# One chunk pair's operands stored quarter by quarter: how they lie in SBUF and how TensorE reads them

## The reference

```
mod = silu(c) @ wmod                      # sa, ca, ga, sb, cb, gb
h = layernorm(x) * (1 + ca) + sa
x = x + ga * attention(h)                 # 2 x 2 scores per feature over the batch
h = layernorm(x) * (1 + cb) + sb
x = x + gb * ((silu(h @ W_gate.T) * (h @ W_up.T)) @ W_down.T)
```

## Time and profile before

| | |
|---|---|
| median of three runs | 2774.9 us |
| the profiled execution's own time | 2773.0 us |
| its span (first to last instruction) | 2771.2 us |
| TensorE matmuls | 11640, busy 98% of the span |
| matmuls of the up projection (lines 1637 to 1639) | 3 x 2416 |
| VectorE, ScalarE busy | 66%, 47% |
| mean granted TensorE clock | 0.992 of 2.4 GHz |
| x_raw loads | 21 of 1024 KB |

### The profile page before, as it was taken

One profiled execution on the slowest core, in us unless ns is written; L12 is line 12 of the kernel. 1 busy time (PEld: TensorE's weight loads), 2 busy tenths in 40 slices (PEclk: granted clock), 3 DMA queues, 4 the chain that ended last, 5 costly groups with the idle time before them and its releaser, 6 DMA issues. The chain is left out here.

```text
span 2771.2 us, 32925 instructions
## 1 busy us (share of the span) xinstructions
PE 2708.4 (98%) x11640; PEld 2145.2 (77%) x11640; DVE 1816.6 (66%) x2503; ACT 1310.3 (47%) x2058; POOL 156.9 (6%) x206
## 2 busy tenths in 40 slices
PE   8989999998999999999999999999999999999999
PEld 3336888887888887888887888887888888888887
DVE  6979778865677766777766666556555555445444
ACT  4657455654456654465654333333433443343342
POOL 5300011000011000010000000000000000000000
PEclk9989999999999999999999999999999999999999
DMA  8683566649665649556658887787757657657655
GB/s 349 232 306 120 194 220 204 201 159 277 194 195 194 215 158 296 177 196 209 206 173 249 266 261 252 261 267 241 279 200 265 239 193 263 242 195 261 249 197 169
DMA packets 322595, 625.32 MB, mean 226 GB/s; under 512 B 22016, under 2 KB 134656, under 8 KB 317312
## 3 DMA queue, kind: packets, MB, share of 16 engines
q1 hardware_dynamic: 304528, 550.85, 59.0%
q0 software_dynamic: 17088, 59.78, 6.5%
q10 hardware_dynamic: 816, 12.58, 1.1%
HBM read 437.79 MB, written 185.34 MB: 225 GB/s over the span
## 5 line engine op out<-in xcount | busy, mean ns | idle before, releaser
L1637 PE MATMUL ps<-x_hi_P,w_hi 128*128 128x512 f32 x2416 | 945.5, 391 | 24.9 <-ACT p L815 14.6
L1638 PE MATMUL ps<-x_lo_P,w_hi 128*128 128x512 f32 x2416 | 943.2, 390 | 0.0
L1639 PE MATMUL ps<-x_hi_P,w_lo_P 128*128 128x512 f32 x2416 | 942.8, 390 | 0.0
L740 ACT CAST w_hi<-w_raw_P 128x512 fp32r<-128x512 f32 x604 | 373.7, 621 | 429.6 <-PE ps L1639 421.6
L1637 PEld LDWEIGHTS ps<-x_hi_P,w_hi 128*128 128x128 f32 x2416 | 455.6, 189 | 124.6 <-ACT p L815 15.8
L1155 DVE TENSOR_TENSOR w_lo_P<-w_raw_P,w_hi 128x512 fp32r<-128x512 f32 x604 | 413.7, 686 | 210.9 <-PE ps L1639 187.2
L1639 PEld LDWEIGHTS ps<-x_hi_P,w_lo_P 128*128 128x128 f32 x2416 | 455.4, 189 | 95.1
L1638 PEld LDWEIGHTS ps<-x_lo_P,w_hi 128*128 128x128 f32 x2416 | 455.8, 189 | 93.5
L1700 PE MATMUL ps<-hh,w_hi 128*128 128x512 f32 x1232 | 480.7, 390 | 6.5 <-DVEq L1356 5.7
L1701 PE MATMUL ps<-hl,w_hi 128*128 128x512 f32 x1232 | 480.2, 390 | 0.0
L1702 PE MATMUL ps<-hh,w_lo 128*128 128x512 f32 x1232 | 480.2, 390 | 0.0
(11 more groups left out here) (181 smaller groups left out, 2120.4 us busy)
## 6 DMA issues: line engine op xcount, KB each, us to landing
w_raw_P<-wgu SPq DMA_DIRECT2D x294, 256.0 KB, 2.9
w_raw_P<-wsum_dram SPq DMA_DIRECT2D x252, 256.0 KB, 3.4
hl_raw<-h_dram SPq DMA_DIRECT2D x84, 768.0 KB, 7.3
w_raw<-wds_dram SPq DMA_DIRECT2D x64, 704.0 KB, 4.6
h_dram<-hb SPq DMA_DIRECT2D x33, 1280.0 KB, 5.5
w_raw<-wdn SPq DMA_DIRECT2D x48, 704.0 KB, 5.0
wsum_dram<-w_raw_P SPq DMA_DIRECT2D x84, 256.0 KB, 2.8
x_raw_P<-xr_dram SPq DMA_DIRECT2D x21, 1024.0 KB, 8.2
```

Source lines behind the costliest of these rows:

```text
L740: s.copy(w_hi[m % HI_RING][:], w_raw[(name, u)][:]).then_inc(whi_ready, 1)
L1637: mm(bank, hi[:, w], x_hi[name][:, k, :], start=fresh and k == 0, stop=False, skip_group_check=not fresh)
L1638: mm(bank, hi[:, w], x_lo[name][:, k, :], start=False, stop=False, skip_group_check=not fresh)
L1639: ins = mm(bank, lo[:, w], x_hi[name][:, k, :], start=False, stop=k == KH - 1, skip_group_check=not fresh)
```

## The change

The load of an x_raw operand no longer puts the four quarters side by side within each feature tile. It copies each quarter's 512 elements per partition as they lie in DRAM, so that in SBUF a partition holds quarter 0 with its four feature tiles, then quarter 1, and so on. The columns of one feature tile are now four runs of 128 at a pitch of 512 elements. For the three later pairs the matmuls take their moving side with that pattern, and their output bank is written as four quarters that follow on one another. For the first pair nothing changes.

```
-  sp.dma_start(x_raw[n][:].rearrange("p k (r t) -> p k r t", r=NGRP),
-               xr_dram[s + 1, PRODUCTS.index(n)].rearrange("r p (k t) -> p k r t", k=KH)).then_inc(
+  sp.dma_start(x_raw[n][:].rearrange("p k t -> p (k t)").rearrange("p (r w) -> p r w", r=NGRP),
+               xr_dram[s + 1, PRODUCTS.index(n)].rearrange("r p w -> p r w")).then_inc(
                 xp_loaded[n], 16)

+            def quarters(bank):
+                return bank.rearrange("p (r t) -> p r t", r=NGRP)
+
+            def operand(x_, s, k):
+                if s == 0:
+                    return x_[:, k, :]
+                return x_[:].rearrange("p k t -> p (k t)").rearrange("p (r k t) -> p r k t", r=NGRP, k=KH)[:, :, k, :]

+                to = quarters(bank) if s else bank
                 for k in range(KH):
                     w = slice(k * P, (k + 1) * P)
-                    mm(bank, hi[:, w], x_hi[name][:, k, :], start=fresh and k == 0, stop=False, skip_group_check=not fresh)
-                    mm(bank, hi[:, w], x_lo[name][:, k, :], start=False, stop=False, skip_group_check=not fresh)
-                    ins = mm(bank, lo[:, w], x_hi[name][:, k, :], start=False, stop=k == KH - 1, skip_group_check=not fresh)
+                    xh, xl = operand(x_hi[name], s, k), operand(x_lo[name], s, k)
+                    mm(to, hi[:, w], xh, start=fresh and k == 0, stop=False, skip_group_check=not fresh)
+                    mm(to, hi[:, w], xl, start=False, stop=False, skip_group_check=not fresh)
+                    ins = mm(to, lo[:, w], xh, start=False, stop=k == KH - 1, skip_group_check=not fresh)
```

## The result

The changed kernel takes 2758.35 us (median of four runs, 2756.08 to 2761.17) against 2774.51 before: a ratio of 0.9945, 95% interval [0.9933, 0.9957], 16.2 us less. The forecast was 2760.

A forecast was written before the change was run, and what follows sets the result against it. TensorE, 98% busy, bounds the kernel and loses 30.1 us at three pair changes. Landings 12.0 plus clock 3 give 15.0 off the profiled 2773.0, hence 2758.0; with 1.9 for the median 2759.9, say 2760 us; range 2750 to 2777.

The forecast's parts named there:

- A load shorter by 0.8 us: The 21 x_raw loads at the three pair changes: 2 KB runs save 0.73 to 0.83 us each, taken as 0.8.
- an estimate of 0.43: Saving per x_raw load in us by the skill page's packet overhead rule, 6.4 us over three places; not adopted.
- P2 lands 4.0 us sooner, and TensorE's P6 with it: At each pair change, P2's operand lands 4.0 us earlier; the large idle time's end moves one for one.
- 5 x 0.8: P2's is the fifth of seven x_raw loads in SP's queue, each 0.8 us shorter, so 4.0 us earlier.
- Some 2.3 us stay idle before P6: TensorE's idle time before P6 at a pair change: from 4.6 us some 2.3 stay, VectorE nearly as late.
- 12.0 us from the landings, 3 of the clock: Gains over the three pair changes: 12.0 us from earlier P2 landings, 3 from TensorE's clock, 15.0 in all.
- The clock term: TensorE's slowed clock after the idle times at the three places: 0 to 7.1 us come back, taken as 3.
- Four runs of 128 columns cost nothing: Moving side of 5436 matmuls in three later pairs: bounds 0 to 221 us, taken as 0.
- Rival D: TensorE pays at each run turn in 5436 matmuls: 2792 at 2 ns a turn, 2966 at most; chance 0.18.
- Rivals B and C: B: stall at the three places goes altogether, 2750, chance 0.08. C: landing hardly moves, 2769 to 2775, chance 0.17.
- Some signs were set wrongly: Signs of being right: x_raw landing delay, packets under 2 KB, P2's cast waits, idle before P6, matmul counts, dense starts.

The follow-up runs named there:

- the half-way point of 1 KB: Changed kernel with x_raw loaded in runs of 1 KB, 1024 runs a load in place of 512: 2763.19 us, ratio 0.9963.
- the runs alone: Kernel before, with its old load of 512 B runs, but TensorE reading four runs of 128 columns and writing four quarters: 2773.72 us, ratio 0.9998.
- the PSUM kernel: Changed kernel's new load, but TensorE reading 512 adjacent columns and writing its PSUM bank in pairs of columns 8 apart: 2760.06 us, ratio 0.9951.

## Why the prediction was right

Point by point, by its own steps:

- *A load shorter by 0.8 us.* 0.87 by the landings of P5 and P6, to which the half-way point of 1 KB (0.57) fits. It is a little more because the long packets were cheaper here than between 400 and 500 us: 1.052 x 16 x 15 / 5.85 = 43 us of packet time a MB and not 49. One premise was wrong without harm: not the destination was cut into pieces but the reading of xr_dram, into the same 2048 runs of 512 B. The rule of the Trainium skill, "DMA: Bandwidth & Descriptors", section "Why small descriptors are slow", had given an estimate of 0.43; the trace does not agree.
- *P2 lands 4.0 us sooner, and TensorE's P6 with it.* 3.9 us at the first place, and the fixed 6.07 us behind it stayed. But not as 5 x 0.8: P1's load landed only 0.4 sooner, of which 0.2 is the lead that the trace had already, P5's and P6's another 0.88 and 0.87, P7's and P2's 1.81 together. Four loads saved 0.9 each and the first next to nothing; why the first did not is not shown. The backlog was real: moving P2's load up by one place moved its landing as well.
- *Some 2.3 us stay idle before P6.* 1.91, 1.92 and 2.00.
- *12.0 us from the landings, 3 of the clock.* The sum was near, but by two errors of opposite sign, which is in part luck. TensorE's idle time before P6 shrank by 2.7, 2.4 and 3.8 us, 8.8 in all. The smaller gaps around it shrank by 1.0 at the first place and grew by 0.2 and 1.3 at the other two (at the third VectorE was late next: it is named at 1520.24). So all idle time in the three stretches went from 60 - 52.07, 60 - 53.96 and 60 - 53.25 to 60 - 55.72, 60 - 56.07 and 60 - 55.71: from 20.7 to 12.5 us, 8.2 less and not 12.0. The clock term was too small: at the first and third place the 2.9 and 2.5 us came back in full, 5.4 in place of 3; at the second nothing did. That makes 13.6 us, where the count of matmuls gives 12.6; the 1 us between is not located. The clock at the second place is also part of why the median gained more than the profiled execution: in the other profile of this kernel it stayed up, and the stretch held nine matmuls more (2.0 us).
- *Four runs of 128 columns cost nothing.* Shown twice, by the runs alone and by 1332 matmuls in 300 us. Rival D's price had its basis in no row, and it exists only for shorter runs.
- *Rivals B and C.* The stall did not go altogether, and the freed engines were not taken by others: the rate rose to 390 GB/s.
- *Some signs were set wrongly.* I expected landing 5.5 to 7.5 us after issue; it is 12.4, up from 8.1. The load of P2 is issued at 650.73 and not 658.93, 8.2 us sooner, nearly all of it from the hold of 8.69 us behind P1's load that is down to 0.33; the landing is set by the backlog, not by the issue. The 220 to 233 matmuls in a stretch were too few for my own sum (5 us a place are 22 more): it is 237 to 242. P2's casts wait 5.03, 5.03 and 6.09 us where I had 3 to 5. Of packets under 2 KB hardly any are left (147), not a quarter. 8.1 us at 311 GB/s are 2.5 MB in flight, 12.4 at 390 are 4.8 MB: with longer runs more bytes were in flight ahead of a load.

## What to carry to other kernels

Where a DMA queue is a backlog, the length of the runs in its loads (here those in which DRAM is read; short runs on the SBUF side were not tried) sets its rate, and the gain of longer runs adds up over the loads ahead of the one that is waited for. Ask of such a transfer when it lands, never how long after its issue: the second number grew by half here while the first improved. Moving the awaited load up the queue is the cheaper edit for the same idle time (9 of the 16 us), and both together end at the next engine's work, here VectorE's. A landing that comes 4 us sooner is not 4 us of TensorE's time: at the three places 3.6, 2.1 and 2.5 us of idle time went, and the clock decided about another 0 to 3 us at each.

## What the runs showed of the hardware

- A matmul of 512 float32 columns that reads four runs of 128 from SBUF goes at the rate of one run, 1332 in 300 us. Runs of 32, 16 and 8 columns cost 237, 242 and 233 ns in place of 226.8, in no order of their length, and single elements 453 and 460 ns at a step of 2 and 4.
- Its PSUM output in pairs of float32 at a pitch of 8 columns costs nothing: again 1332 in 300 us.
- Packets of 512 B, 1 KB and 2 KB in a full queue gave 4.26, 3.69 and 3.39 us for 1.25 MB, of which 0.25 MB were in packets of 2 KB each time.
- How far SP's queue ran ahead depended on the length of the runs: issue to landing of a 1 MB load was 8.1 us with 512 B, 10.0 with 1 KB and 12.4 with 2 KB, while the landing itself came sooner.
- An idle time of TensorE of 1.9 to 2.4 us brought the clock to 1.2 GHz at one of the six places of the changed kernel's two profiles (after a wait of 1.92 us, and not after 2.35), and at two of three in the PSUM kernel's (after 2.04 and 2.25 us, not after 1.90), so the length of the wait alone does not tell; one of 4.3 to 5.8 us did at all three places before.
